# Second attention layer of a decoder: value products gathered at the end of a group, three dense PSUM banks in turn

## The chip, the cores and the metric

The kernel runs as one launch on one core of a Trainium2 chip. The core has a matrix engine (TensorE; PE for its matmuls, PEld for its weight loads), VectorE (DVE), ScalarE (ACT), GpSimd (POOL), SyncE (SP, which here starts DMAs), an on-chip memory of 128 partitions, and an accumulator memory, PSUM, with eight banks. The metric is device time in microseconds; lower is better.

## The reference, cut to what matters

A batch is 16 sequences of 224 rows of 512 numbers. Layer 1 is a quantised self-attention and layer 3 an attention with a mixture of experts; neither is touched. The change is all in layer 2, a cross attention of 16 heads of 32 over a context of 750 rows:

```python
q = (Q @ Wq + bq).reshape(B, L, H, E)      # B=16, L=224, H=16, E=32
k = (K @ Wk + bk).reshape(B, S, H, E)      # S=750, K = V = ctx_1024
v = (V @ Wv + bv).reshape(B, S, H, E)
scores = jnp.einsum('blhe,bshe->bhls', q, k)
A = jax.nn.softmax(scale * scores, axis=-1)
out = jnp.einsum('bhls,bshd->blhd', A, v).reshape(B, L, H * E)
return out @ We + be                        # then x = layernorm(x + that)
```

## The kernel before, in words

Layer 2 runs over the 16 batches in an unrolled loop. Each batch has four **groups** of four heads, since a head's 32 channels take a quarter of the 128 partitions. A group needs, on TensorE:

- four **row-max** products (`row_max`, L1439), each 112 queries by 376 keys for four heads into PSUM banks 0 to 3; VectorE reduces each to maxima (`reduce_max`, L1618). They are made one group ahead.
- the maxima transposed (unit M, L1370), copied by ScalarE (L1553).
- three **score** products (`scores`, L1449 and L1453), each 250 keys by 224 queries for four heads, into the same banks 0 to 3; ScalarE takes the exponential (L1583).
- three **value** products (`values`, L1461), which sum exponentials times value rows over the keys, and two **ones** products (`sums`, L1468), which sum the exponentials themselves after GpSimd has added them pairwise (L1347, L1352). Both go to bank 6 or 7, as the group is even or odd. VectorE then takes the reciprocal and multiplies (`attend`, L1630 and L1631) into `out_T`.

Row-max and score products share banks 0 to 3, so they alternate: row-max, VectorE reduces, scores, ScalarE exponentiates, row-max. While VectorE or ScalarE has those banks, TensorE does **dense** work of a neighbouring batch, set by hand in the table `WINDOWS`: C (transposes of 125 context rows, or of 112 rows of x for C6 and C7; eight a batch), Q (four), K (eight), VV (value rows, twelve), O (the output projection of the batch before; two of 112 rows by 512 columns). Dense units and M take banks 4 and 5 in turn by their place in `ORDER`. ScalarE copies a dense result (the high part for C, Q, K; all of it for VV), and VectorE then writes the low-order rest (`unit` in the vector block: C L1600, Q L1604, K L1608; O L1614). A unit waits until its bank's earlier unit has been emptied (`emptied`, `earlier_in_bank`).

One group on TensorE is: row-max 0, M, slot 0, the last ones product of the group before, then for t = 0, 1, 2: scores t, slot 2t+1, row-max t+1, slot 2t+2, values t; the first ones product follows values 2. A group so has seven slots of dense work.

`first()` makes everything of batch 0 ahead of the loop; `final()` makes the last output. In batch 0 there is no O, in batch 15 no work for a next batch. SyncE stores a finished batch, then loads the rows of the context and of x of a later batch, then the rows `y2` to which an output is added; all these go out in that order. GpSimd adds the bias row to `y2` at a batch's start (L1341).

## Time and profile before

| what | value |
|---|---|
| median of three timed runs | 4292.89 us (4291.1 to 4294.06) |
| the profiled execution | 4295.02 us, its span 4293.1 us |
| PE, PEld, DVE, ACT, POOL busy over the span | 81%, 58%, 59%, 38%, 20% |
| mean granted TensorE clock | 0.876 of full speed |
| batches of layer 2 | from some 1366 us to 2879 us of the span |

A PE row's duration runs from a matmul's start to its modelled end and overlaps the next row, so the cost of a stretch is read from start to start of neighbouring rows. "x16" means sixteen instructions merged in one row; a float32 product appears as two instructions. The names say what is written and read; Wv, Wk, Wq tell the units VV, K and Q apart.

### The profile page before, as it was taken

Reading aid. Unit: us, or ns where it says so; the run is one execution under the profiler, and the core shown is the slowest. Engines: PE = TensorE matmul, PEld = TensorE weight load, DVE = VectorE, ACT = ScalarE, POOL = GpSimd, SP = SyncE. Lnnn points to the kernel's source line nnn. Section 1 sums busy time; section 2 is a strip of 40 time slices with the busy share of each in tenths; the row PEclk is TensorE's granted clock in tenths of the full one; section 3 lists DMA queues with packets and bytes.
Section 4 is the critical chain, followed back from the end, with each engine's and each line's share of the span. In section 5 each row is a group of like instructions: output and inputs, shape, how many; then the busy total and the mean of one; then the engine's idle time right before and its main releaser. Section 6 shows DMA issues by size and latency. Waiting matters only on the chain. (4 is left out here: it accounts for less than half of the span.)

```text
span 4293.1 us, 76365 instructions
## 1 busy us (share of the span) xinstructions
PE 3463.3 (81%) x30658; PEld 2482.2 (58%) x30658; DVE 2514.2 (59%) x3799; ACT 1626.5 (38%) x3064; POOL 873.9 (20%) x710
## 2 busy tenths in 40 slices
PE   0787753279647999999999999959994299999994
PEld 0343321146226777777777777735552298999993
DVE  8679889989863555555555555527764133333333
ACT  2222279968023333333333333313221133333332
POOL 0000012200001333343333334320001411111110
PEclk9998875555778999999999999969996599999997
DMA  3500033333051110000111000012100533433325
GB/s 152 182 1 1 15 112 105 95 94 95 0 181 45 40 36 29 29 29 29 33 37 43 29 29 29 10 39 64 40 21 36 190 83 84 93 86 84 83 44 151
DMA packets 140172, 276.51 MB, mean 64 GB/s; under 512 B 43464, under 2 KB 43464, under 8 KB 135776
## 3 DMA queue, kind: packets, MB, share of 16 engines
q1 hardware_dynamic: 124208, 239.60, 17.7%
q0 software_dynamic: 14592, 30.44, 4.1%
q8 instruction: 234, 3.83, 0.4%
q10 hardware_dynamic: 1072, 2.10, 0.2%
q14 instruction: 66, 0.54, 0.0%
HBM read 158.02 MB, written 102.23 MB: 61 GB/s over the span
## 5 line engine op out<-in xcount | busy, mean ns | idle before, releaser
L1618 DVE TENSOR_REDUCE arena<-psum 112x4 f32<-112x1504 f32 x256 | 440.3, 1720 | 303.2 <-PE psum L1439 302.7
L1583 ACT ACTIVATE arena<-psum 125x1792 f32<-125x1792 f32 x192 | 320.3, 1668 | 289.3 <-PE psum L1453 289.3
L1347 POOL TENSOR_TENSOR arena<-arena 125x896 f32<-125x896 f32 x128 | 270.1, 2110 | 680.9 <-ACT arena L1583 680.9
L1352 POOL TENSOR_TENSOR arena<-arena 125x896 f32<-125x896 f32 x128 | 269.3, 2104 | 292.4 <-ACT arena L1583 287.4
L2367 POOL DMA_INDIRECT x_plus_h_rows<-arena x72 | 114.6, 1592 | 731.7 <-DVE arena L2538 727.4
L2528 DVE TENSOR_TENSOR gelu_T_rest<-arena,gelu_T_high 128x384 fp32r<-128x384 f32 (+1 forms) x192 | 104.6, 547 | 269.5 <-ACT gelu_T_high L2474 269.5
L2389 PE MATMUL psum<-tokens_T_high,w_high 128*128 128x384 f32 (+1 forms) x768 | 255.6, 333 | 1.6 <-DVE tokens_T_rest L2503 1.6
L2391 PE MATMUL psum<-tokens_T_high,w_rest 128*128 128x384 f32 (+1 forms) x768 | 254.9, 332 | 0.0
L2390 PE MATMUL psum<-tokens_T_rest,w_high 128*128 128x384 f32 (+1 forms) x768 | 254.7, 332 | 0.0
L1608 DVE SCALAR_TENSOR_TENSOR k_T_rest<-psum,arena,k_T_high 128x376 fp32r<-128x376 f32 x128 | 77.9, 609 | 287.1 <-ACT k_T_high L1564 287.1
L821 ACT ACTIVATE arena<-arena,scales 112x224 bf16<-112x224 uint8 x512 | 238.5, 467 | 2.5
L760 PE MATMUL psum<-arena 64*112 64x224 bf16 x512 | 79.2, 410 | 191.2 <-DVE arena L780 178.5
L1360 PE MATMUL psum<-Wv_high,ctx_T_high 128*125 128x256 f32 x768 | 231.3, 301 | 0.0
L2389 PE MATMUL psum<-w_high,gelu_T_high 128*128 128x512 f32 (+1 forms) x576 | 228.7, 397 | 0.0
L2469 ACT ACTIVATE arena<-psum 128x384 f32<-128x384 f32 (+1 forms) x192 | 92.6, 482 | 354.3 <-PE psum L2391 352.7
L2391 PE MATMUL psum<-w_high,gelu_T_rest 128*128 128x512 f32 (+1 forms) x576 | 224.9, 390 | 0.0
L2390 PE MATMUL psum<-w_rest,gelu_T_high 128*128 128x512 f32 (+1 forms) x576 | 224.3, 389 | 0.0
L1361 PE MATMUL psum<-Wv_rest,ctx_T_high 128*125 128x256 f32 x768 | 215.5, 281 | 0.0
L1362 PE MATMUL psum<-Wv_high,ctx_T_rest 128*125 128x256 f32 x768 | 215.5, 281 | 0.0
L1461 PE MATMUL psum<-arena 125*32 125x224 f32 x3072 | 190.9, 367 | 5.4 <-ACT arena L1583 5.4
L1360 PE MATMUL psum<-ctx_T_high,Wk_high 128*128 128x376 f32 x512 | 184.1, 360 | 0.0
L1361 PE MATMUL psum<-ctx_T_rest,Wk_high 128*128 128x376 f32 x512 | 171.2, 334 | 0.0
(361 smaller groups left out, 8680.8 us busy)
## 6 DMA issues: line engine op xcount, KB each, us to landing
arena<-L_ffn_moe_w SPq DMA_DIRECT2D x16, 2048.0 KB, 10.9
arena<-ctx SPq DMA_DIRECT2D x16, 1500.0 KB
rows_by_slot<-arena SPq DMA_DIRECT2D x1, 18200.0 KB, 52.1
arena<-x SPq DMA_DIRECT2D x14, 1024.0 KB, 13.1
arena<-arena SPq DMA_DIRECT2D x16, 896.0 KB, 7.0
arena<-x_after_attn SPq DMA_DIRECT2D x32, 448.0 KB, 16.2
dots_ints<-arena SPq DMA_DIRECT2D x16, 784.0 KB, 4.8
arena<-dots_ints SPq DMA_DIRECT2D x16, 784.0 KB, 5.7
```

The source lines that it names most:

```text
L821: last = S.activation(junk[:, pr % 2, j, :], d8[:, u, h, (j % 2) * NS:(j % 2 + 1) * NS], ACT.Exp, scale=col("minus_s_d")[0:HALF], accum_ou ...
L1347: G.tensor_tensor(some_exps[:, r, :, :], prob[:, t, :, 0:NS], prob[:, t, :, NS:2 * NS], ALU.add).then_inc(paired, 1)
L1352: G.tensor_tensor(some_exps[:, 0, :, :], some_exps[:, 0, :, :], prob[:, 1, :, s * NS:(s + 1) * NS], ALU.add).then_inc(paired, 1)
L1360: PE.matmul(to, wh(k), xh(k), start=(k == 0), stop=False)
L1361: PE.matmul(to, wh(k), xl(k), start=False, stop=False)
L1362: last = PE.matmul(to, wl(k), xh(k), start=False, stop=(k == KC - 1))
L1461: last = PE.matmul(psum[DH2 * j:DH2 * (j + 1), 6 + g % 2, 0:NS], vR[:, u, mt, h * DH2:(h + 1) * DH2], prob[:, t, j, s * NS:(s + 1) * NS], ...
L1583: S.activation(prob[:, t, :, :], score_psum(MC, 2 * NS), ACT.Exp, scale=SCALE2).then_inc(exp_done, 1)
L1618: return V.tensor_reduce(rmx[:, i // 2, i % 2, :], score_psum(HALF, HC), axis=AX.X, op=ALU.max).then_inc(r_free, 1)
L2389: PE.matmul(to, wh(k), xh(k), start=(k == 0), stop=False)
L2390: PE.matmul(to, wh(k), xl(k), start=False, stop=False)
L2391: last = PE.matmul(to, wl(k), xh(k), start=False, stop=(k == n - 1))
```

## The change

Value and ones products of a group all come after its last row-max product, in one run, into bank 6 for every group. Bank 7 joins 4 and 5 as a dense bank; a unit's bank is its place in `ORDER` modulo three, and a unit waits for the one three places earlier. `None` entries pad `ORDER` so that banks fit. A group has six slots; `WINDOWS` is rewritten so that each batch's same C, Q, K and VV units stand in them, and O is cut into four units of 112 rows by 256 columns, spread over groups 0 to 2. `out_T` is doubled, so that the next batch's groups don't overwrite what O still reads. On VectorE, `attend` comes ahead of slot 0's units, and a row maximum comes ahead of the rests of the slot before it (but behind an O); the three small operations of `combine` follow the last row maximum directly. GpSimd adds the bias row after its first addition of a batch. SyncE stores a batch when four O units are read, so after the last slot of group 2 of the next batch (before: slot 5 of group 0).

```diff
-        o2T = sb("out_T", [P, NG2, NS], F32, L2)
+        o2T = sb("out_T", [P, 2, NG2, NS], F32, L2)
...
+        NO2 = 4
         WINDOWS = (
-            (((Q, 3),), ((K, 6),), ((K, 7),), ((O, 0),), ((C, 0), (C, 1)), ((O, 1),), ((C, 2), (C, 3))),
-            (((C, 4), (C, 5)), ((K, 0),), ((C, 6), (C, 7)), ((K, 1),), ((VV, 0),), ((VV, 1), (VV, 2)), ((Q, 0),)),
-            (((Q, 1),), ((K, 2),), ((VV, 3),), ((K, 3),), ((VV, 4),), ((VV, 5),), ((VV, 6),)),
-            (((Q, 2),), ((K, 4),), ((VV, 7),), ((K, 5),), ((VV, 8),), ((VV, 9), (VV, 10)), ((VV, 11),)),
+            (((K, 6),), ((K, 7),), ((Q, 3), (C, 0)), ((O, 0),), ((VV, 0), (C, 1)), ((VV, 1), (C, 2))),
+            (((VV, 2), (C, 3)), ((O, 1),), ((VV, 3), (C, 4)), ((K, 0),), ((VV, 4), (C, 5)), ((VV, 5), (C, 6))),
+            (((VV, 6), (C, 7)), ((K, 1),), ((O, 2),), ((VV, 7), (Q, 0)), ((K, 2),), ((O, 3),)),
+            (((K, 3),), ((VV, 8), (Q, 1)), ((K, 4),), ((VV, 9), (Q, 2)), ((K, 5),), ((VV, 10), (VV, 11))),
         )
+        DENSE_BANKS = (4, 5, 7)
+        NDB = len(DENSE_BANKS)
+        VALUE_BANK = 6
...
         def bank(unit):
-            return 4 + ORDER.index(unit) % 2
+            return DENSE_BANKS[ORDER.index(unit) % NDB]
...
                         for g in range(NG2):
-                            last = PE.matmul(psum[0:HALF, at, :], o2T[:, g, i * HALF:(i + 1) * HALF], We[:, g, :], start=(g == 0), stop=(g == NG2 - 1))
+                            last = PE.matmul(psum[0:HALF, at, 0:DV2], o2T[:, u, g, rows], We[:, g, cols], start=(g == 0), stop=(g == NG2 - 1))
...
+                        def values_and_sums():
+                            pe.wait_ge(attended, n + 2)
+                            if g == 0:
+                                pe.wait_ge(v_moved, b * NV2 + NV2)
+                            for t in range(TP):
+                                pe.wait_ge(exp_done, n * TP + (t + 1))
+                                values(u, g, t)
+                            for r in range(ROUNDS):
+                                sums(n, g, r)
                         next_max(0)
                         dense((M, g), b, b_next, b_before, u, first, last)
                         slot(0)
-                        if not (first and g == 0):
-                            sums(n - 1, (g - 1) % NG2, 1)
                         for t in range(TP):
                             next_scores(t)
                             slot(2 * t + 1)
                             next_max(t + 1)
-                            slot(2 * t + 2)
-                            next_values(t)
+                            if t < TP - 1:
+                                slot(2 * t + 2)
+                        values_and_sums()
...
                         for t in range(TP):
-                            slot(2 * t + 1)
+                            of_output = [what for what in WINDOWS[g][2 * t + 1] if what[0] == O]
+                            others = [what for what in WINDOWS[g][2 * t + 1] if what[0] != O]
+                            empty(of_output)
                             if more:
                                 reduce_max(n + 1, t + 1)
-                            slot(2 * t + 2)
-                        if more:
-                            combine(n + 1, ch)
+                                if t == TP - 1:
+                                    combine(n + 1, ch)
+                            empty(others)
+                            if t < TP - 1:
+                                empty(WINDOWS[g][2 * t + 2])
```

TensorE at the end of a group, before: the last value product (L1461; waits for the exponential, x2_exp), the first ones product (L1468), row-max 0 (L1439), M (L1370).

```order
L1461 MATMUL psum<-arena 32x224 [waits x2_exp]
L1461 MATMUL psum<-arena 32x224 x7
L1468 MATMUL psum<-arena,ones 32x224 [waits x2_ps]
L1468 MATMUL psum<-arena,ones 32x224 x3
L1439 MATMUL psum<-k_T_high,q_T_high 112x376 [waits x2_rfr,x2_kmv,x2_qmv]
L1439 MATMUL psum<-k_T_high,q_T_high 112x376 x3
L1439 MATMUL psum<-k_T_rest,q_T_high 112x376 x4
L1439 MATMUL psum<-k_T_high,q_T_rest 112x376 x4
L1370 MATMUL psum<-identb,arena 128x112 [waits x2_nmx,x2_vmv]
L1370 MATMUL psum<-identb,arena 128x112
```

The same place in the change, from the first value product (L1477) on; L1484 is the ones product, L1455 the row-max.

```order
L1477 MATMUL psum<-arena 32x224 [waits x2_exp,x2_att]
L1477 MATMUL psum<-arena 32x224 x7
L1477 MATMUL psum<-arena 32x224 [waits x2_exp]
L1477 MATMUL psum<-arena 32x224 x7
L1477 MATMUL psum<-arena 32x224 [waits x2_exp]
L1477 MATMUL psum<-arena 32x224 x7
L1484 MATMUL psum<-arena,ones 32x224 [waits x2_ps]
L1484 MATMUL psum<-arena,ones 32x224 x3
L1484 MATMUL psum<-arena,ones 32x224 [waits x2_ps]
L1484 MATMUL psum<-arena,ones 32x224 x3
L1455 MATMUL psum<-k_T_high,q_T_high 112x376 [waits x2_rfr,x2_kmv,x2_qmv]
L1455 MATMUL psum<-k_T_high,q_T_high 112x376 x3
```

Value products 0 and 1 and the second ones product have moved here; they stand in one unbroken run.

TensorE ahead of scores 0, before: the last matmul of a Q unit (L1362), the second ones product (L1468), the scores (L1449).

```order
L1362 MATMUL psum<-x_T_high,Wq_rest 128x224
L1468 MATMUL psum<-arena,ones 32x224 [waits x2_ps]
L1468 MATMUL psum<-arena,ones 32x224 x3
L1449 MATMUL psum<-q_T_high,k_T_high 125x224 [waits x2_tmv,x2_rfr]
L1449 MATMUL psum<-q_T_high,k_T_high 125x224 x3
L1449 MATMUL psum<-q_T_rest,k_T_high 125x224 x4
```

The same place in the change: the last matmul of a K unit (L1377), the scores (L1465).

```order
L1377 MATMUL psum<-ctx_T_high,Wk_rest 128x376
L1465 MATMUL psum<-q_T_high,k_T_high 125x224 [waits x2_tmv,x2_rfr]
L1465 MATMUL psum<-q_T_high,k_T_high 125x224 x3
L1465 MATMUL psum<-q_T_rest,k_T_high 125x224 x4
L1465 MATMUL psum<-q_T_high,k_T_rest 125x224 x4
```

Scores now follow dense work directly, with no product in tiles of 32 columns between.

VectorE in group 3, before: row maximum L1618, rests of Q L1604 and K L1608, `attend` L1630 and L1631, `combine` L1623 to L1625.

```order
L1618 TENSOR_REDUCE arena<-psum 112x4 [waits x2_rmm]
L1604 SCALAR_TENSOR_TENSOR q_T_rest<-psum,arena,q_T_high 128x224 [waits x2_qhi]
L1630 RECIPROCAL arena<-psum 128x224 [waits x2_sum]
L1631 TENSOR_TENSOR arena<-psum,arena 128x224 [waits x2_dch]
L1608 SCALAR_TENSOR_TENSOR k_T_rest<-psum,arena,k_T_high 128x376 [waits x2_khi]
L1618 TENSOR_REDUCE arena<-psum 112x4 [waits x2_rmm]
L1608 SCALAR_TENSOR_TENSOR k_T_rest<-psum,arena,k_T_high 128x376 [waits x2_khi]
L1618 TENSOR_REDUCE arena<-psum 112x4 [waits x2_rmm] x2
L1623 TENSOR_TENSOR arena<-arena 112x8 [waits x2_rfr]
L1624 TENSOR_SCALAR arena<-arena 112x8 [waits x2_dch]
L1625 SCALAR_TENSOR_TENSOR arena<-arena 112x8 [waits x2_dch]
```

The same group in the change: row maximum L1636, `attend` L1648 and L1649, rests of K L1625 and Q L1621, `combine` from L1641.

```order
L1636 TENSOR_REDUCE arena<-psum 112x4 [waits x2_rmm]
L1648 RECIPROCAL arena<-psum 128x224 [waits x2_sum]
L1649 TENSOR_TENSOR arena<-psum,arena 128x224 [waits x2_dch]
L1625 SCALAR_TENSOR_TENSOR k_T_rest<-psum,arena,k_T_high 128x376 [waits x2_khi]
L1636 TENSOR_REDUCE arena<-psum 112x4 [waits x2_rmm]
L1621 SCALAR_TENSOR_TENSOR q_T_rest<-psum,arena,q_T_high 128x224 [waits x2_qhi]
L1625 SCALAR_TENSOR_TENSOR k_T_rest<-psum,arena,k_T_high 128x376 [waits x2_khi]
L1636 TENSOR_REDUCE arena<-psum 112x4 [waits x2_rmm]
L1621 SCALAR_TENSOR_TENSOR q_T_rest<-psum,arena,q_T_high 128x224 [waits x2_qhi]
L1625 SCALAR_TENSOR_TENSOR k_T_rest<-psum,arena,k_T_high 128x376 [waits x2_khi]
L1636 TENSOR_REDUCE arena<-psum 112x4 [waits x2_rmm]
L1641 TENSOR_TENSOR arena<-arena 112x8 [waits x2_rfr]
```

The row maximum has moved ahead of the rests that wait for ScalarE, `attend` ahead of the first rest.

## Rows read from the trace of the kernel before

**Rows 1.** windows view (us; busy PE, PEld, DVE, ACT, POOL; clock, DMA share, GB/s), second layer

```profile
2039.00:2146.00 107.00, 105.35 (x1320) 77.18 (x1316) 58.69 (x72) 41.57 (x57) 40.06 (x19) 1.00 0.11 33
```

**Rows 2.** timeline of ACT (start us, us, engine line op): two copies of group 0's maxima

```profile
1458.86 0.35 ACT L1553 COPY arena<-psum 128x224 bf16<-128x224 bf16 x1 [1.81 <-PE psum L1370]
...
2778.98 0.35 ACT L1553 COPY arena<-psum 128x224 bf16<-128x224 bf16 x1 [1.81 <-PE psum L1370]
```

**Rows 3.** timeline of PE from 2017 us: first instruction of each stretch

```profile
2017.02 0.38 PE L1360 MATMUL psum<-Wv_high,ctx_T_high 128*125 128x256 f32 x1
...
2020.06 0.43 PE L1439 MATMUL psum<-k_T_high,q_T_high 32*112 32x376 f32 x4
...
2020.77 0.38 PE L1360 MATMUL psum<-Wv_high,ctx_T_high 128*125 128x256 f32 x1
...
2022.37 0.96 PE L1461 MATMUL psum<-arena 125*32 125x224 f32 x16
2023.15 0.56 PE L1468 MATMUL psum<-arena,ones 125*32 125x224 f32 x8
2023.64 0.43 PE L1439 MATMUL psum<-k_T_high,q_T_high 32*112 32x376 f32 x4
...
2024.36 0.27 PE L1370 MATMUL psum<-identb,arena 112*128 112x112 bf16 x2
2024.44 0.35 PE L1360 MATMUL psum<-x_T_high,Wq_high 128*128 128x224 f32 x1
...
2025.95 0.58 PE L1468 MATMUL psum<-arena,ones 125*32 125x224 f32 x8
2026.47 0.37 PE L1449 MATMUL psum<-q_T_high,k_T_high 32*125 32x224 f32 x4
...
2027.51 0.44 PE L1360 MATMUL psum<-ctx_T_high,Wk_high 128*128 128x376 f32 x1
...
2029.76 0.43 PE L1439 MATMUL psum<-k_T_high,q_T_high 32*112 32x376 f32 x4
...
2034.65 3.69 PE L1403 MATMUL psum<-arena 128*112 128x512 f32 x8
2038.27 0.43 PE L1439 MATMUL psum<-k_T_high,q_T_high 32*112 32x376 f32 x4
...
2038.98 1.07 PE L1382 MATMUL psum<-ident,arena 125*128 125x125 f32 x8
2039.98 0.96 PE L1461 MATMUL psum<-arena 125*32 125x224 f32 x16
2040.87 0.38 PE L1449 MATMUL psum<-q_T_high,k_T_high 32*125 32x224 f32 x4
```

**Rows 4.** waits view, 1950 to 2136 us (us in total, times, longest)

```profile
PEld psum L1370 <- DVE ctx_T_rest L1600: 1.9, 2, 0.9
```

**Rows 5.** timeline of all engines, batch 0, a stretch after scores without dense work

```profile
1376.04 0.37 PE L1449 MATMUL psum<-q_T_high,k_T_high 32*125 32x224 f32 x4
...
1378.92 0.43 PE L1439 MATMUL psum<-k_T_high,q_T_high 32*112 32x376 f32 x4 [1.76 <-ACT arena L1583]
```

**Rows 6.** timeline of DVE, 2020 to 2031 us: a row maximum and a rest of K

```profile
2020.88 1.72 DVE L1618 TENSOR_REDUCE arena<-psum 112x4 f32<-112x1504 f32 x1 [5.17 <-PE psum L1439]
...
2030.48 0.61 DVE L1608 SCALAR_TENSOR_TENSOR k_T_rest<-psum,arena,k_T_high 128x376 fp32r<-128x376 f32 x1 [1.60 <-ACT k_T_high L1564]
```

**Rows 7.** page, part 5: the additions on POOL (xcount, busy, mean ns)

```profile
L1347 POOL TENSOR_TENSOR arena<-arena 125x896 f32<-125x896 f32 x128 | 270.1, 2110 | 680.9 <-ACT arena L1583 680.9
```

**Rows 8.** DMA view, 1948 to 2000 us (KB each, median us to landing)

```profile
arena<-x_after_attn SPq DMA_DIRECT2D x2, 448.0 KB, 15.8
xattn_rows<-arena SPq DMA_DIRECT2D x1, 448.0 KB, 3.1
```

**Rows 9.** timeline of PE, the second pair of transposes before batch 0

```profile
1308.20 1.93 PE L1382 MATMUL psum<-ident,arena 125*128 125x125 f32 x8 [0.55 <-DVE ctx_T_rest L1600]
```

**Rows 10.** windows view, the last batch, columns as in Rows 1

```profile
2804.00:2827.00 23.00, 16.24 (x210) 9.96 (x210) 8.86 (x10) 5.00 (x4) 8.37 (x4) 0.55 0.01 1
```

More of the change, by code:

```diff
@@ L1244, in bank @@
         def bank(unit):
-            return 4 + ORDER.index(unit) % 2
+            return DENSE_BANKS[ORDER.index(unit) % NDB]
         def earlier_in_bank(unit, first, last):
-            at = ORDER.index(unit) - 2
-            while at >= 0 and not present(ORDER[at], first, last):
-                at -= 2
+            at = ORDER.index(unit) - NDB
+            while at >= 0 and (ORDER[at] is None or not present(ORDER[at], first, last)):
+                at -= NDB
             if at >= 0:
@@ L1255, in earlier_in_bank, with last_in_bank @@
                 return None, 0
-            at = len(ORDER) + ORDER.index(unit) - 2 - 2 * (ORDER.index(unit) // 2)
+            at += len(ORDER)
+            assert ORDER[at] is not None and ORDER[at][0] != O
             return ORDER[at], 1
+        def last_in_bank(i):
+            at = len(ORDER) - NDB + i
+            while ORDER[at] is None or not present(ORDER[at], False, True):
+                at -= NDB
+            return ORDER[at]
         with phase("x2", "c", "x", "y0", "y1", "yb", "cmm", "chi", "clo", "qmm", "qhi", "qmv", "kmm", "khi", "kmv", "vmm", "vmv", "rmm", "rfr", "nmx", "tmm", "tmv",
@@ L1430, in dense @@
                         emptied(*earlier, batch_of(earlier, b_before, b, b_next))
-                    unit(kind, i, bank(what), batch_of(what, b_before, b, b_next), u)
+                    unit(kind, i, bank(what), batch_of(what, b_before, b, b_next), 1 - u)
                 def row_max(g, i):
@@ L1467, in sums @@
                     for j in range(GH):
-                        last = PE.matmul(psum[DH2 * j:DH2 * (j + 1), 6 + g % 2, NS:2 * NS], ones[0:MC, 0:DH2], some_exps[:, r, j, :],
+                        last = PE.matmul(psum[DH2 * j:DH2 * (j + 1), VALUE_BANK, NS:2 * NS], ones[0:MC, 0:DH2], some_exps[:, r, j, :],
                                          start=False, stop=(r == ROUNDS - 1))
@@ L1539, in final @@
                 def final():
-                    sums(NB * NG2 - 1, NG2 - 1, 1)
-                    for i in range(2):
-                        if i == 0:
-                            pe.wait_ge(o_read, 2 * NB - 2)
-                            pe.wait_ge(t_moved, NB * NG2)
-                        unit(O, i, 4 + i, NB - 1, 1)
+                    for i in range(NO2):
+                        if i < NDB:
+                            earlier = last_in_bank(i)
+                            emptied(*earlier, batch_of(earlier, NB - 2, NB - 1, None))
+                        else:
+                            emptied(O, i - NDB, NB - 1)
+                        unit(O, i, DENSE_BANKS[i % NDB], NB - 1, 1)
                 loop(pe, first, body, final)
@@ L1584, in body @@
                             slot(2 * t + 1)
-                            slot(2 * t + 2)
+                            if t < TP - 1:
+                                slot(2 * t + 2)
                 def first():
                     for i, (kind, j) in enumerate(FIRST):
-                        unit(kind, j, 4 + i % 2, 0, 0)
+                        unit(kind, j, DENSE_BANKS[i % NDB], 0, 0)
                 loop(act, first, body, lambda: None)
@@ L1637, in body, with empty @@
                         ch = Chain(dve, dch, n * 3 + 2) if not first or g else Chain(dve, dch, 2)
-                        def slot(i):
-                            for what in WINDOWS[g][i]:
+                        def empty(some):
+                            for what in some:
                                 if present(what, first, last):
@@ L1664, in first @@
                     for i, (kind, j) in enumerate(FIRST):
-                        unit(kind, j, 4 + i % 2, 0, 0)
+                        unit(kind, j, DENSE_BANKS[i % NDB], 0, 0)
                     for i in range(4):
@@ L1671, in final @@
                     dve.wait_ge(attended, NB * NG2 + 1)
-                    attend(NB * NG2 - 1, NG2 - 1, Chain(dve, dch, (NB * NG2 - 1) * 3 + 3))
-                    for i in range(2):
-                        unit(O, i, 4 + i, NB - 1, 1)
+                    attend(NB * NG2 - 1, NG2 - 1, 1, Chain(dve, dch, (NB * NG2 - 1) * 3 + 3))
+                    for i in range(NO2):
+                        unit(O, i, DENSE_BANKS[i % NDB], NB - 1, 1)
                 loop(dve, first, body, final)
```

48 lines of the change are left out of this document (22 added, 26 removed).

## The prediction

> **What bounds the kernel now.** I read the windows first. Inside layer 2 TensorE is busy 105.35 of 107 us at granted clock 1.00, while VectorE has 58.69, ScalarE 41.57 and GpSimd 40.06 [rows 1]. So a middle batch lasts as long as TensorE's own work, its changes from one kind of product to another, and what it waits for. Next the timeline of ScalarE gives the length of a batch: its copies of the maxima of group 0 lie at 1458.86 (batch 1) and 2778.98 (batch 15), so the 14 batches between take 94.29 us each [rows 2]. Then TensorE's timeline, from start to start [rows 3]: a stretch of two VV 3.04, of one 1.60; K 2.25; Q 1.51; two C 1.00; O 3.62; row-max 0.71; M 0.08; scores 1.04; values 0.89 when scores follow and 0.78 when ones follow; ones 0.49 behind values and 0.52 alone.
>
> The second VV costs 1.44, so opening and closing a dense stretch costs 3.04 - 2 x 1.44 = 0.16. Without it a unit costs K 2.09, Q 1.35, C 0.42, O 3.46. A batch of before is then: 8 K 16.72, 12 VV 17.28, 4 Q 5.40, 8 C 3.36, 2 O 6.92, 4 M 0.32, 16 row-max 11.36, 12 scores 12.48, the values and ones of four groups 4 x (0.89 + 0.89 + 0.78 + 0.49 + 0.52) = 14.28, and 28 dense stretches x 0.16 = 4.48; together 92.60. The measured 94.29 leaves 1.69 us of waits. The waits view shows the largest: twice in two batches the M of group 1 stands 0.95 us behind VectorE's rest of a C unit, its bank's earlier user [rows 4].
>
> **The change part by part, in a middle batch.**
>
> Dense stretches. They go from 28 to 24: 4 x 0.16 = -0.64. The number of K, VV, Q and C units is the same. A stretch that now touches scores directly (12 a batch) has no example in a steady batch; dense next to values and dense next to row-max cost alike, so I take the same 0.16. Its bounds are 0.08 (half a change) and 0.24, thus 1.0 us a batch either way.
>
> Values and ones. In one run they pay for one opening and one closing. Closing towards scores is 0.89 - 0.78 = 0.11, so eight ones instructions without it are 0.49 - 0.11 = 0.38 and sixteen values instructions in the middle of a run 0.76. The run is 0.78 + 0.76 + 0.76 + 0.38 + 0.49 = 3.17 against 3.57: four groups -1.60. Bounds are 3.0 (ones as short as the rows' overlap would let them be) and 3.57 (nothing saved).
>
> O. Its columns stay the same, its instructions go from 16 to 32. A VV instruction of 256 columns takes 1.44 / 12 = 0.12, of which 0.107 are its columns at 2.4 GHz; 16 more at 0.013 are +0.2. The page "TensorEngine Tiling (Array Packing)" of the Trainium skill, section "Instruction Overhead", has about 60 cycles on each matmul; as an estimate by that rule the sixteen would add 0.4 us, and the end would be 3 us later than mine. VV's step contradicts 60 cycles on top of the columns, so I don't use it.
>
> The old waits. 1.69 goes, if three banks remove it. With two banks a unit waits for the one two before; M of group 1 stood directly behind a pair of C. With three, and with C never next to C, each unit's predecessor has at least one whole stretch of banks 0 to 3 between. So -1.69, with bounds 0 and -1.69.
>
> New waits. Two floors must be covered by every dense stretch. After scores: with no dense work scores to row-max takes 2.88 [rows 5], less 1.04 leaves 1.84. After row-max: the reduction starts 0.82 after the products and lasts 1.72 [rows 3, 6], so scores can follow 2.54 after row-max began, less 0.71 leaves 1.83. The thinnest stretches now are an O quarter, 3.46 / 2 + 0.2 / 4 + 0.16 = 1.94, Q3 with C0, 1.93, and VV with C, 2.02: all above both floors, but by 0.1. This holds only if the reduction starts at once. Before, it could stand behind a rest that waits for ScalarE (0.61 for K [rows 6]); it now comes ahead of these. That delays the emptying: the rest of K7 ends 2.54 + 0.61 = 3.15 after row-max 1 began and O0, which takes its bank, starts at 0.71 + 1.93 + 1.04 = 3.68. V5 behind the rest of K0 is the same case. I allow +0.1 for all of it.
>
> The run of values waits for nothing new: the third exponential ends before row-max 3. Its second ones product needs an addition on GpSimd (2.11 [rows 7]) which starts when that exponential ends; TensorE comes to it 0.71 + 0.78 + 1.52 + 0.38 = 3.4 later, so 1.2 us are spare. The reduction of row-max 3 (2.54) hides beneath the run, and so do the three small operations ahead of M. `attend` (reciprocal and product, unchanged) comes earlier by one rest, and delays only that rest, whose bank is asked for three units later.
>
> The queues. O3 is read about 62 us into a batch (by the prices above, groups 0 and 1 take 43 and group 2 up to its last slot 19); only then SyncE stores, issues the context and x loads that stand behind, and last y. The store lands in 3.1 and the loads of x and y in 15.8 [rows 8], so y is there some 20 us later. GpSimd asks for it about 36 us after O3: 28 to the end of the batch, then row-max, M, K6, scores, the exponential and one addition of 2.11. The next C needs its rows at about the same time. Cost 0, with 16 us to spare.
>
> Sum of a middle batch: -0.64 - 1.60 + 0.2 - 1.69 + 0.1 = -3.63; 14 of them -50.8.
>
> The ends. Before batch 0, transposes in pairs wait 0.55 for a bank three times [rows 9]; with three banks that goes: -1.7. Batch 0 has no O. Before, its two empty O stretches shrank from 3.62 to the floor, 3.5 us; now four stretches of 1.94 shrink by 0.1 each. So it gains almost nothing more than 3.63 - 3.5 and I take -0.5. Batch 15 has hardly any dense work, and TensorE's granted clock there is 0.55 [rows 10], near its lower level of 1.2 GHz. At the full clock: O leaves two waits of group 0 that it overfilled, -3.5; the values of three groups, which lay in time that was empty anyway, are now 3.17 in a lump instead of 1.27, +5.7; in group 3 two value products (0.89) leave the chain between exponentials, -1.8; sum +0.4. At the half clock the four O quarters overfill their waits by 1.8 each and the lumps double: up to +12. I take +2.
>
> Total: -50.8 - 0.5 - 1.7 + 2 = -51. From the profiled execution's own 4295.02 that is 4244.0. That execution stands 2.1 above the median of the timed runs (4292.89), so I say **4242 us**.
>
> **The rivals.**
>
> A, *the banks come back too late*. For it: row maxima now go first on VectorE, the stretches stand 0.1 above the floors, O0 and V5 have 0.5 to spare. Against it: ScalarE and VectorE are idle more than half of the time. If three places a batch wait 0.5 each, that is 1.5 x 14 = 21: 4263.
>
> B, *the run saves nothing*: the change from one kind of product to another is inside a value product anyway, and the ends of dense stretches toward scores cost more. Then only the waits go: 1.69 x 14 + 2 = 26, 4268. Against it: 0.78 against 0.89 is there in every group.
>
> C, *the second ones product stands on GpSimd*. Place: the end of each group. Before, a whole dense stretch lay between its addition and its product; now 1.2 us do. For it: in group 0 GpSimd has the bias row to add too. Against it: about 6.5 us lie between two exponentials, GpSimd has at most 4.3 of additions in that time. It turns the sum when GpSimd is late by more than 1.2 + 3.6 / 4 = 2.1 in each group; at 3 late the batch loses 7.2, less 3.6 is +3.6 x 14 = 50 above the median of before: 4343, slower.
>
> D, *y comes too late* for GpSimd, which holds all additions behind it. It costs nothing below 36 us from O3 to landing, turns the sum at 40; at 45 a batch loses 9 - 3.6, so +75 on the median of before: 4368. Against it are the 20 us above.
>
> **How the numbers follow.** Forecast 0.66; A 0.17; B 0.08; C 0.05; D 0.02; all rest 0.02. The boundary of dense and scores (1.0 a batch, 14 us), the ends (-3 to +12) and A's sum make the range: low 4225 (all boundaries cheap), high 4266. A measurement of this kernel can tell 0.2% from no change, 8.6 us. Forecast, A and B are all faster by more; a mixture of B with a slow batch 15 comes near zero. Faster 0.88, same 0.05, slower 0.07.
>
> **What would show it.** Right: batches of about 90.7 us between the copies of group 0's maxima; a run of values and ones of some 3.2 from its first start to row-max 0; M directly behind row-max in each group; no wait of L1385 on a rest; dense stretches with K 2.25 as before, beside scores too. A is right if TensorE's weight loads of O, VV or scores wait on VectorE's rests or reductions; B if the run takes 3.5 or K before scores 2.4; C if ones (L1484) wait for GpSimd; D if GpSimd's first long idle of a batch ends at a DMA. I am wrong in the main if batches stay above 92.5.

## The result, and the profile after

| kernel | median, us | lowest to highest | against before |
|---|---|---|---|
| before | 4293.48 (4 runs) | 4291.1 to 4295.32 | |
| changed | 4236.80 (4 runs) | 4233.41 to 4245.45 | ratio 0.9874, 95% interval 0.9861 to 0.9886 |

The change saves 56.7 us, 1.3%. The prediction said 4242, with a range of 4225 to 4266. The spans of the profiled executions are 4293.1 and 4236.8, apart by 56.3.

The windows view of the changed kernel, the stretch that answers to [rows 1]:

```profile
2039.00:2146.00 107.00, 107.00 (x1421) 87.09 (x1420) 59.10 (x73) 43.14 (x59) 40.80 (x20) 1.00 0.10 29
```

TensorE has no idle time left there: 107.00 of 107 us busy at clock 1.00, against 105.35. The timeline of ScalarE, copies of group 0's maxima (L1569 now), answers to [rows 2]; the first is batch 0's:

```profile
1360.57 0.35 ACT L1569 COPY arena<-psum 128x224 bf16<-128x224 bf16 x1 [13.22 <-PE psum L1385]
...
1458.66 0.35 ACT L1569 COPY arena<-psum 128x224 bf16<-128x224 bf16 x1 [4.41 <-PE psum L1385]
...
2724.73 0.35 ACT L1569 COPY arena<-psum 128x224 bf16<-128x224 bf16 x1 [4.41 <-PE psum L1385]
```

Batches 1 to 14 take (2724.73 - 1458.66) / 14 = 90.43 us each; before 94.29, foretold 90.66. TensorE's timeline, the end of group 0 and the start of group 1 of such a batch, answers to [rows 3] (L1375 dense, L1397 transposes C, L1465 scores, L1455 row-max, L1477 values, L1484 ones, L1385 M, L1419 O):

```profile
1922.45 0.39 PE L1375 MATMUL psum<-Wv_high,ctx_T_high 128*125 128x256 f32 x1
...
1923.98 0.59 PE L1397 MATMUL psum<-ident,arena 125*128 125x125 f32 x4
1924.50 0.38 PE L1465 MATMUL psum<-q_T_high,k_T_high 32*125 32x224 f32 x4
...
1925.54 0.39 PE L1375 MATMUL psum<-Wv_high,ctx_T_high 128*125 128x256 f32 x1
...
1927.08 0.59 PE L1397 MATMUL psum<-ident,arena 125*128 125x125 f32 x4
1927.60 0.43 PE L1455 MATMUL psum<-k_T_high,q_T_high 32*112 32x376 f32 x4
...
1928.30 2.48 PE L1477 MATMUL psum<-arena 125*32 125x224 f32 x48
1930.60 0.94 PE L1484 MATMUL psum<-arena,ones 125*32 125x224 f32 x16
1931.47 0.43 PE L1455 MATMUL psum<-k_T_high,q_T_high 32*112 32x376 f32 x4
...
1932.17 0.27 PE L1385 MATMUL psum<-identb,arena 112*128 112x112 bf16 x2
1932.26 0.36 PE L1375 MATMUL psum<-Wv_high,ctx_T_high 128*125 128x256 f32 x1
...
1933.76 0.59 PE L1397 MATMUL psum<-ident,arena 125*128 125x125 f32 x4
1934.28 0.37 PE L1465 MATMUL psum<-q_T_high,k_T_high 32*125 32x224 f32 x4
...
1935.32 1.98 PE L1419 MATMUL psum<-arena 128*112 128x256 f32 x8
1937.23 0.43 PE L1455 MATMUL psum<-k_T_high,q_T_high 32*112 32x376 f32 x4
```

VV with C takes 2.05 (1922.45 to 1924.50), dense next to scores costs no more than next to row-max (2.06 from 1925.54 to 1927.60), an O quarter 1.91, the run of values and ones 3.17 (1928.30 to 1931.47). M follows row-max after 0.70. No start stands behind a wait. In the waits view of two batches what is left of VectorE's reductions is

```profile
PEld psum L1465 <- DVE arena L1636: 2.0, 10, 0.3
```

Before, the same view (1950 to 2136 us) had 22 such entries:

```profile
PEld psum L1449 <- DVE arena L1618: 8.3, 22, 0.6
```

These are waits of weight loads, and most of them cost nothing: the pieces' sum left only 1.69 us a batch for all waits.

Where the 56.3 us of span went, from the rows that mark the ends (TensorE's first transposes at 1305.71 and 1303.87, the last store's issue at 2878.72 and 2822.66):

| stretch | before | changed | difference | foretold |
|---|---|---|---|---|
| up to layer 2's first transpose | 1305.71 | 1303.87 | -1.8 | 0 |
| to batch 0's copy of maxima | 60.59 | 56.70 | -3.9 | -1.7 |
| batch 0 | 92.56 | 98.09 | +5.5 | -0.5 |
| batches 1 to 14 | 1320.12 | 1266.07 | -54.1 | -50.8 |
| batch 15 to the last store | 99.74 | 97.93 | -1.8 | +2 |

The 0.2 us that are missing to 56.3 lie behind layer 2. The first line is code that the change doesn't touch; in the eleven experiments below it lies between 1.2 us above before and 6.2 us below, so it is noise. So runs are compared below by the length of their own stretches.

### The profile page after: what moved, and what is told of

Its sections match the earlier page's. It is cut to its first block and busy times, and to the rows that moved or that the text cites. A ratio compares the mean times of both kernels' runs of the same rounds, so it can differ in the third digit from the quotient of the medians.

```text
span 4236.8 us, 76941 instructions
## 1 busy us (share of the span) xinstructions
PE 3414.0 (81%) x30914; PEld 2544.5 (60%) x30914; DVE 2515.7 (59%) x3831; ACT 1629.3 (38%) x3064; POOL 873.8 (21%) x710
## 5 line engine op out<-in xcount | busy, mean ns | idle before, releaser
L1636 DVE TENSOR_REDUCE arena<-psum 112x4 f32<-112x1504 f32 x256 | 441.6, 1725 | 531.0 <-PE psum L1455 531.0
L1359 POOL TENSOR_TENSOR arena<-arena 125x896 f32<-125x896 f32 x128 | 269.8, 2108 | 830.6 <-ACT arena L1599 637.5
L1599 ACT ACTIVATE arena<-psum 125x1792 f32<-125x1792 f32 x192 | 320.3, 1668 | 160.7 <-PE psum L1469 160.7
L1375 PE MATMUL psum<-Wv_high,ctx_T_high 128*125 128x256 f32 x768 | 233.0, 303 | 0.0
L1377 PE MATMUL psum<-Wv_high,ctx_T_rest 128*125 128x256 f32 x768 | 217.0, 283 | 0.0
L1375 PE MATMUL psum<-ctx_T_high,Wk_high 128*128 128x376 f32 x512 | 183.4, 358 | 0.0
L760 PEld LDWEIGHTS psum<-arena 64*112 64x112 bf16 x512 | 34.2, 187 | 236.4 <-DVE arena L780 223.2
L1377 PE MATMUL psum<-ctx_T_high,Wk_rest 128*128 128x376 f32 x512 | 171.2, 334 | 0.0
```

Source lines behind the costliest of these rows:

```text
L1359: G.tensor_tensor(some_exps[:, r, :, :], prob[:, t, :, 0:NS], prob[:, t, :, NS:2 * NS], ALU.add).then_inc(paired, 1)
L1375: PE.matmul(to, wh(k), xh(k), start=(k == 0), stop=False)
L1377: last = PE.matmul(to, wl(k), xh(k), start=False, stop=(k == KC - 1))
L1599: S.activation(prob[:, t, :, :], score_psum(MC, 2 * NS), ACT.Exp, scale=SCALE2).then_inc(exp_done, 1)
L1636: return V.tensor_reduce(rmx[:, i // 2, i % 2, :], score_psum(HALF, HC), axis=AX.X, op=ALU.max).then_inc(r_free, 1)
```

## The experiments

All times "batch" are the mean of batches 1 to 14 by the same two copies of maxima. Before is 94.29, the changed kernel 90.43.

**e1, two dense banks.**

```diff
-        DENSE_BANKS = (4, 5, 7)
+        DENSE_BANKS = (4, 5)
```

> The changed kernel with two dense banks (4 and 5) in turn instead of three; order, values in one run and O in quarters stay. Theory: three banks matter at two places of a middle batch, read from the changed kernel's trace: C0 would stand behind the rest of K7 (ends 1919.2, C0 starts 1918.28: about 1.0 us) and C5 behind the rest of K0 (ends 1946.3, C5 starts 1945.51: about 0.9). So a middle batch goes from 90.43 to 92.3 us, and the transposes before batch 0 from 7.8 to 10.8; 4236.8 + 14 x 1.9 + 3 = about 4267. Rival: the new order alone took the waits away, the third bank does nothing in the loop: batch 90.4, total about 4240. Second rival: every unit meets a wait somewhere, batch 94 or more, total above 4285.

Measured: 4268.93 us (ratio to before 0.994, 0.9924 to 0.9957), batch 92.42, +1.99. The waits view of two batches, weight loads of the transposes:

```profile
PEld psum L1397 <- DVE k_T_rest L1625: 3.8, 4, 1.0
```

Four waits of 0.95 in two batches, all of C units behind rests of K, as the theory named them (C0 behind K7, C5 behind K0).

**e2, value products apart.** `next_values(t)` makes value product t, and behind the third both ones products (before, the second of them stood behind slot 0 of the next group).

```diff
                             next_max(t + 1)
                             if t < TP - 1:
                                 slot(2 * t + 2)
-                        values_and_sums()
+                            next_values(t)
```

> The changed kernel with value products 0 and 1 put back behind slots 2 and 4, value product 2 and both ones products at the end; three banks and six slots stay. Theory (a change between kinds of product costs what the rows say): each of the two costs 0.89 instead of 0.76, so +0.13 x 8 = +1.0 a middle batch, 91.5 us; the last batch gains some 5 since two of its value products again lie in empty time; about 4236.8 + 15 - 5 = 4247. Rival B of the prediction (a run saves nothing): batch 90.4, about 4232. Rival: the run's place, not its length, matters (a reduction or exponential was hidden less well before), batch above 92.5.

Measured: 4278.35 us (ratio 0.9958, 0.9944 to 0.9972), batch 93.24, +2.81 and not +1.0. TensorE's timeline at the end of group 1 of a middle batch (L1455 row-max, L1477 values, L1484 ones), and VectorE's beneath it (L1637 row maximum):

```profile
1970.57 0.43 PE L1455 MATMUL psum<-k_T_high,q_T_high 32*112 32x376 f32 x4
...
1971.28 0.96 PE L1477 MATMUL psum<-arena 125*32 125x224 f32 x16
1972.06 1.19 PE L1484 MATMUL psum<-arena,ones 125*32 125x224 f32 x16
1973.27 0.43 PE L1455 MATMUL psum<-k_T_high,q_T_high 32*112 32x376 f32 x4
```

```profile
1971.40 1.72 DVE L1637 TENSOR_REDUCE arena<-psum 112x4 f32<-112x1504 f32 x1 [3.25 <-PE psum L1455]
```

Three value products cost 0.89 + 0.89 + 0.78 = 2.56 in place of 2.30, the +1.04 a batch that the theory had. But ones now take 1.21 (1972.06 to 1973.27) in place of 0.87: row-max 0 may start only when the reduction of row-max 3 has ended, at 1971.40 + 1.72 = 1973.12, and 0.78 + 0.87 don't cover it. That is 0.34 to 0.36 in each group, 1.4 a batch. Another 0.3 stands behind M of group 2. The new table has no slot behind row-max 3, so the run at the end is what hides that reduction; its place weighs as much as its being one piece. So the theory and its last rival both hold a part.

**e3, the kernel before with three dense banks.**

```diff
-            return 4 + ORDER.index(unit) % 2
+            return DENSE_BANKS[ORDER.index(unit) % NDB]
...
-                                pe.wait_ge(attended, n + 1)
+                                pe.wait_ge(attended, n + 2)
```

`DENSE_BANKS` is (4, 5, 7), and values and ones of every group go to bank 6, so value product 0 now waits for the `attend` of the group before (second edit).

> The kernel before with dense banks 4, 5 and 7 in turn and bank 6 for all values; its order, seven slots and VectorE order stay. Theory: of the 1.69 us of waits a batch only those on a bank go: M of group 1 (0.7 more than usual) and the transposes behind it (0.2 to 0.4), so a batch of 93.2 us; what stays is 0.24 at a lone VV after scores (the exponential's floor) and 0.21 where a reduction stands behind rests. Prologue 3 shorter. 4293.5 - 14 x 1.1 - 3 = about 4275. Rival: all waits were bank waits, batch 92.6, about 4267. Second rival: single value bank makes value product 0 wait for attend: batch above 94.3.

Measured: 4285.65 us (ratio 0.9975, 0.9965 to 0.9985), batch 94.07, only -0.22. TensorE's timeline, row-max 0 and M (L1383) of group 1:

```profile
1951.04 0.43 PE L1452 MATMUL psum<-k_T_high,q_T_high 32*112 32x376 f32 x4
...
1952.46 0.26 PE L1383 MATMUL psum<-identb,arena 112*128 112x112 bf16 x2 [0.65 <-DVE arena L1637]
```

M starts 1.42 after row-max 0, where 0.71 is normal, as before, and what it waits for is L1637, the last operation of `combine`, not a bank. The theory is refuted: the largest old wait was VectorE's order. The third bank does take away the waits at the C units of group 1, but behind C6 and C7 the scores now wait for a row maximum (L1630), which stands behind other work of VectorE:

```profile
1960.33 0.37 PE L1462 MATMUL psum<-q_T_high,k_T_high 32*125 32x224 f32 x4 [0.42 <-DVE arena L1630]
```

**e4, the changed kernel with VectorE's order of before** (`combine` stays behind the last row maximum; the first line of the edit stands ahead of `attend`).

```diff
+                        empty(WINDOWS[g][0])
...
-                            empty(of_output)
+                            empty(WINDOWS[g][2 * t + 1])
                             if more:
                                 reduce_max(n + 1, t + 1)
...
-                            empty(others)
```

> The changed kernel with VectorE's order of before: a slot's rests ahead of the row maximum that follows it, attend behind the rests of slot 0. Theory: where K stands in the slot after scores its rest ends about 0.45 later than the reduction could start; that shows where the next stretch is thin: Q3 with C0, O2, VV4 with C5, 0.2 to 0.4 each, so about +0.9 a batch, 91.3, total about 4250. Rival: the stretches cover it, batch 90.4, total 4237. Second rival: attend's delay holds a bank and M or K wait, batch above 92.5.

Measured: 4253.43 us (ratio 0.9907, 0.9891 to 0.9924), batch 91.43, +1.00. Q3 with C0 takes 2.30 in place of 1.96. O2 takes 2.31 (from 1964.25) in place of 1.91, and the scores behind it wait for the row maximum:

```profile
1966.56 0.38 PE L1465 MATMUL psum<-q_T_high,k_T_high 32*125 32x224 f32 x4 [0.33 <-DVE arena L1636]
```

VV4 with C5 takes 2.31 in place of 2.06. All three places and sizes are those expected.

**e5, all three undone: the table of six slots is left** (edits of e1, e2 and e4 together, and `combine` last; O stays in quarters, and both ones products stay behind value product 2).

> The changed kernel with only its new table of six slots (and O in quarters, out_T doubled, GpSimd's order) left: two dense banks, value products 0 and 1 apart, VectorE's order of before, combine last. Theory (the three aids each carry weight only because the stretches are thinner): undone one by one they cost 1.99, 2.81 and 1.00 us a middle batch; together 90.43 + 5.8 = about 96.2, slower than the 94.29 of before, total about 4325. Rival (each aid saves by itself, six slots save their 0.64 in any case): batch 93 to 94, total 4275 to 4290.

Measured: 4286.94 us (ratio 0.9987, 0.9978 to 0.9997), batch 93.80. The theory is refuted, the costs don't add: undone alone they are 1.99, 2.81 and 1.00, together 3.37. Next to e2 the banks and VectorE's order are worth only 93.80 - 93.24 = 0.56. TensorE's rows show why. VectorE's old order writes the rest of K ahead of the row maximum, so C0 behind K7 and C5 behind K0 start at once with two banks too: Q3 ahead of C0 takes 1.44, where in e1 it took 2.42 with the wait. The row maxima that this delays lie ahead of scores 1 and 2, beneath a value product of 0.89. What is left stands at the end of groups 0 and 1, where a rest of C goes ahead of the reduction of row-max 3. Timeline of TensorE and of VectorE at the end of group 0:

```profile
1948.67 1.18 PE L1484 MATMUL psum<-arena,ones 125*32 125x224 f32 x16
1950.36 0.43 PE L1455 MATMUL psum<-k_T_high,q_T_high 32*112 32x376 f32 x4 [0.52 <-DVE arena L1637]
```

```profile
1947.91 0.68 DVE L1618 TENSOR_TENSOR ctx_T_rest<-psum,ctx_T_high 128x500 fp32r<-128x500 f32 x1 [3.29 <-ACT ctx_T_high L1574]
1948.50 1.71 DVE L1637 TENSOR_REDUCE arena<-psum 112x4 f32<-112x1504 f32 x1
```

The ones take 1.69 here and 1.60 in group 1, against 1.21 to 1.23 in e2 and 0.87 in the changed kernel. The 94.29 - 93.80 = 0.49 that e5 saves against before is a balance: four stretches fewer -0.64, ones in one piece -0.56 (4 x (1.01 - 0.87)), the old waits -1.69, O in quarters +0.08, the ones' new waits +2.25; together -0.56.

**e6, the kernel before with `combine` directly behind the last row maximum.**

```diff
                                 reduce_max(n + 1, t + 1)
+                                if t == TP - 1:
+                                    combine(n + 1, ch)
                             slot(2 * t + 2)
-                        if more:
-                            combine(n + 1, ch)
```

> The kernel before with one edit: the three small operations of combine stand directly behind the last row maximum, ahead of the rests of slot 6. Theory: the 0.7 us that M of group 1 waited was for these, behind the rests of C2 and C3, not for a bank; group 0 to 1 goes from 25.55 to about 25.0 with two banks (M then waits for its bank's rest of C2, some 0.15), a batch 93.8, total about 4287. Rival (the prediction's reading, a bank wait): no change, 94.3.

Measured: 4291.42 us (ratio 0.9993, 0.9984 to 1.0003, which is no difference that the times can show); batch 94.16. TensorE's timeline at the same place:

```profile
1952.81 0.43 PE L1439 MATMUL psum<-k_T_high,q_T_high 32*112 32x376 f32 x4
...
1953.66 0.27 PE L1370 MATMUL psum<-identb,arena 112*128 112x112 bf16 x2
1954.24 1.07 PE L1382 MATMUL psum<-ident,arena 125*128 125x125 f32 x8 [0.31 <-DVE ctx_T_rest L1600]
```

M starts 0.85 after row-max 0 and not 1.41, and from group 0's M to group 1's it is 25.00 in place of 25.55, as the theory said. But C4 behind it waits 0.31 for the rest of its bank's C unit, and the next group is 0.43 longer (23.29 against 22.86). Here two waits lay over one another: the order of VectorE and the bank. Removing the first shows the second.

**e7, the first row-max products between the value rows.** Before batch 0 each of group 0's four row-max products stands ahead of three VV.

```diff
                     for i, (kind, j) in enumerate(FIRST):
+                        if kind == VV and j % (NV2 // 4) == 0:
+                            m = j // (NV2 // 4)
...
+                            row_max(0, m)
```

> The changed kernel with another order before batch 0: the four row-max products of group 0 stand each ahead of three VV units instead of behind all twelve. Theory: three reductions of 2.54 us, which left TensorE idle, go beneath the VV units: -9.5; and TensorE's clock, which fell in that idle time (K6 of batch 0 took 3.41 instead of 2.24), stays up: -1.5 more. Total 4236.8 - 11 = about 4226, middle batches 90.43. Rival: batch 0 waits for something else anyway (table load of the exponential, ScalarE's copies), total about 4232.

Measured: 4228.28 us (ratio 0.9849, 0.9833 to 0.9866), 8.5 below the changed kernel's median. From the first transpose to the copy of maxima 49.6 in place of 56.7: -7.1, less than the 9.5. (The intervals of the two ratios touch; it is this stretch that tells the kernels apart.) Batch 0 didn't gain, 98.45: K6 took 2.24, but group 0's ones products now waited for GpSimd twice, 1.65 and 1.45, where the changed kernel waits 1.44 once, and the clock fell behind that.

**e8, the bias row back at the head of a batch** (GpSimd's order of before).

> The changed kernel with GpSimd's addition of the bias row back at the head of a batch. Theory: GpSimd's first tensor operation of the layer starts some 7 us after it could (in batch 0 the first addition of exponentials began at 1374.5, its exponential ended at 1367.4); at the head of batch 0 this is hidden as before, so ones 2 of group 0 doesn't wait 1.4 and VectorE's small operation of 2.02 takes 0.2: batch 0 shorter by 1.5 to 2, middle batches 90.43, total 4235. Rival: y now is asked for before it has landed in every batch, batches above 91.

Measured: 4235.42 us (ratio 0.9869, 0.9852 to 0.9885), batch 0 97.92, middle batches 90.43. Ones 2 of group 0 no longer waits, yet batch 0 loses 0.2 us and not 1.5 to 2. In this profiled run the clock fell once more, right behind the empty O place of group 1 (VV took 2.72 in place of 1.54; the granted clock from 1390 to 1394 us is 0.57, where the changed kernel has 1.00). y is never late.

**e9, the value products of the last batch alone apart.**

> The changed kernel with value products 0 and 1 of the last batch alone back behind slots 2 and 4 (the other batches keep their run). Theory: in batch 15 the slots are nearly empty, so the two products lie in time in which TensorE waits, and the run that three groups put on the chain (3.3 us at half clock) shrinks; -5, total about 4232. Rival: the short run leaves the last reduction bare and the clock falls further, 4236 to 4240.

Measured: 4240.65 us (ratio 0.9876, 0.9861 to 0.9892), not told apart from the changed kernel. Batch 15 to the last store is 94.90 in place of 97.93, -3.0 and not -5; batch 0, untouched, was 101.3 in this profiled run in place of 98.1. So in total it is inconclusive, and the mechanism shows in its own stretch. The 101.3 also says how far a length of batch 0 can be trusted: the same code took 98.1 in one profiled execution and 101.3 in another, so the 0.2 of e8 and the 1.0 of e10 below are no differences by themselves.

**e10, batch 0's empty O places filled** with products of We that nobody reads.

```diff
                         def slot(i):
+                            if first and not any(present(w, first, last) for w in WINDOWS[g][i]):
+                                what = WINDOWS[g][i][0]
...
+                                count = 1 if last and i % 2 == 0 else 3
+                                for k in range(count):
+                                    PE.matmul(psum[0:HALF, bank(what), 0:DV2], We[:, k, 0:HALF], We[:, k, 0:DV2], start=(k == 0), stop=(k == count - 1))
```

> The changed kernel with each of batch 0's four empty O places filled by three float32 products of We with itself (256 columns, about 1.4 us, read by nobody, overwritten by the bank's next unit). Theory: batch 0 takes 98.1 against 90.4 of a middle batch because TensorE's idle 1.8 us at these places lets the granted clock fall (VV 2.61 instead of 1.53, values 3.72 instead of 2.30); filled, batch 0 takes 93.5 to 94.5, total about 4233. Rival: the floors and GpSimd's late start make it, and filling changes nothing or adds: 4237 to 4239.

Measured: 4240.09 us (ratio 0.9884, 0.9868 to 0.9899), batch 0 97.06, -1.0. By itself it does nothing that the times show. But the filling does what it was meant to do, and GpSimd takes the gain away. Windows view of e10 behind the ones products of group 0 and at the O place of group 2 (1417 us), where the changed kernel's clock is 0.57:

```profile
1387.00:1390.00 3.00, 3.00 (x24) 2.55 (x19) 2.13 (x2) 0.34 (x1) 0.00 (x0) 0.50 0.03 5
1417.00:1421.00 4.00, 3.64 (x50) 3.00 (x49) 1.80 (x2) 1.50 (x1) 0.52 (x1) 1.00 0.58 183
```

The clock no longer falls at the O places, and the value products of group 2 take 2.29. It falls in group 0, where TensorE now waits for GpSimd twice (3.39 us in all, against 1.44 once):

```profile
1384.18 0.58 PE L1484 MATMUL psum<-arena,ones 125*32 125x224 f32 x8 [1.94 <-POOL arena L1367]
1386.22 0.59 PE L1484 MATMUL psum<-arena,ones 125*32 125x224 f32 x8 [1.45 <-POOL arena L1359]
```

So the rival's number came out, but not its reason.

**e11, all of e7 to e10, and batch 15's empty slots filled as well.**

> First maxima between the values, bias row first, values of the last batch apart, and empty slots filled with such products of We in batch 0 and batch 15 (three after scores, one after row-max). Theory: -8.5 (run e7) - 1.4 (e8) - 4 (batch 0 at full clock) - 5 (e9) and in batch 15 the half clock goes, 3.12 + 3.74 per pair of row-max and scores becomes 2.6 + 2.9, some 1.4 x 11 = -15: about 4203. Rival: the fillers stand in the chain and the clock does not rise: above 4222.

Measured: 4213.00 us (ratio 0.9816, 0.9803 to 0.9830), 23.8 below the changed kernel. Batch 0 takes 90.61, batch 15 to the last store 85.65, middle batches 90.43. The windows view (columns as in [rows 1]) of batch 0 and batch 15, of the changed kernel and then of e11:

```profile
1361.00:1459.00 98.00, 89.07 (x1162) 72.73 (x1162) 48.07 (x56) 37.72 (x50) 35.93 (x17) 0.94 0.07 22
2725.00:2823.00 98.00, 71.05 (x877) 49.45 (x875) 36.13 (x42) 22.70 (x19) 35.69 (x17) 0.77 0.02 6
```

```profile
1355.00:1445.00 90.00, 88.43 (x1180) 72.01 (x1172) 46.78 (x55) 37.61 (x50) 36.02 (x17) 1.00 0.07 24
2721.00:2807.00 86.00, 66.26 (x848) 42.81 (x840) 29.78 (x35) 20.61 (x15) 31.84 (x17) 0.95 0.09 23
```

The granted clock is 1.00 in place of 0.94 in batch 0 and 0.95 in place of 0.77 in batch 15. In batch 0 the parts need each other: e7, e8 and e10 alone each left a fall of the clock, in e7 and e10 behind the waits for GpSimd that e8's order removes, in e8 behind the empty O places that e10 fills. Which smaller set would be enough wasn't run.

## Why the prediction was right, point by point

- *Dense stretches*, -0.64. Dense next to scores costs what dense elsewhere does, 0.09 to 0.10 at each end; VV with C 2.05 against the 2.02 used. The term was not measured by itself; e5's balance fits with it to 0.07.
- *Values and ones*, -1.60. The run takes 3.17, to the hundredth the sum of its pieces. The prediction names that the reduction of row-max 3 hides beneath the run, but gives it no price: with the run in pieces it is bare, 1.4 us a batch (e2).
- *O*, +0.2. A quarter takes 1.91 against 1.94; four of them 7.64 against 7.24 for two halves, 0.32 of which are the two more stretches, so +0.08. An O instruction of 256 columns takes (1.91 - 0.16) / 8 = 0.219 us, half of the 0.43 of one of 512, so nearly all of it goes by columns. The rule of about 60 cycles on each matmul (the Trainium skill, "TensorEngine Tiling (Array Packing)", section "Instruction Overhead"), read as the prediction read it, on top of the columns, makes +0.4 as an estimate; the measured +0.08 decides against that reading.
- *The old waits*, -1.69: the size holds, since nothing is left of them, but the step's reason failed, and that the number fits all the same is luck. The prediction read [rows 4], a wait of M's weight load on its bank, and gave the whole credit to the third bank. The row of M's matmul in the same trace of before names another:

```profile
1955.63 0.26 PE L1370 MATMUL psum<-identb,arena 112*128 112x112 bf16 x2 [0.64 <-DVE arena L1625]
```

M waited for `combine`, which stood behind the rests of C2 and C3, with a bank wait hidden just beneath (e6); the third bank alone gives 0.22 (e3). By TensorE's rows in a batch of before, 1.56 of the 1.69 stood at four places: 0.71 at this M, 0.18 at the C units behind it, 0.42 at C6 and C7 and the value product behind them, and 0.25 at a lone VV behind scores, whose stretch of 1.60 is shorter than its floor. In e5, with two banks, VectorE's old order and `combine` last, the only starts that wait in the middle batch read (1922 to 2018 us) are those of row-max 0: it is the new table that takes the old waits away. The third bank is worth 1.99 for another reason: it removes waits that the new table makes under VectorE's new order (e1).
- *New waits*, +0.1: none. The floor after scores held (2.88 less 1.04 in batch 0). The one after row-max came out at 1.90 and not 1.83 (row-max at 1413.32 to scores at 1415.93 over the empty O2 place of batch 0, 2.61 less 0.71), so O2 with its 1.91 covers it by 0.01 and not by 0.1; that nothing waits there is close to luck. e4 shows that they bind as soon as a reduction starts 0.4 late. Rival A is thus right in its mechanism and wrong in this kernel, because VectorE's new order prevents it.
- *Queues*. y and the context rows were in time in all batches; rival D is out. Rival C happened once, in batch 0: timeline of ScalarE, of GpSimd and of TensorE (L1599 exponential, L1359 addition, L1484 ones).

```profile
1365.70 1.67 ACT L1599 ACTIVATE arena<-psum 125x1792 f32<-125x1792 f32 x1
```

```profile
1374.53 2.10 POOL L1359 TENSOR_TENSOR arena<-arena 125x896 f32<-125x896 f32 x1 [193.16 <-issue]
...
1383.16 2.08 POOL L1359 TENSOR_TENSOR arena<-arena 125x896 f32<-125x896 f32 x1
```

```profile
1385.29 0.58 PE L1484 MATMUL psum<-arena,ones 125*32 125x224 f32 x8 [1.44 <-POOL arena L1359]
```

GpSimd's first addition starts 7.2 us after the exponential ended at 1367.37, and its last one so late that the second ones product waits 1.44.

- *The ends* are where the numbers were wrong. The way to batch 0 gained 3.9 and not 1.7: from the first transpose to Q0 went from 10.80 to 7.79. The prediction added up three idle entries of 0.55 [rows 9], but such an entry starts at the modelled end of a matmul, which overlaps the next; from start to start a pair had taken 2.49 (1308.20 less 1305.71), and from the first start to the modelled end of the last all eight units took 9.4 before and take 6.4 now. Batch 0 was forecast by its floors alone, at one clock; this is the step that was wrong in size and in kind. By its rows, against a middle batch of 90.43, it takes 1.6 more at K6 and K7 (3.41 and 2.67), whose clock fell while TensorE waited for the reductions ahead of batch 0, 1.6 at the ones product that waits for GpSimd, and 4.7 in the work right behind three of the four empty O places (before there were two places), where the clock is 0.57 to 0.59. e10 confirms the last term: with these places filled the clock stays at 1.00 there. TensorE's timeline, group 2 of batch 0:

```profile
1427.32 0.43 PE L1455 MATMUL psum<-k_T_high,q_T_high 32*112 32x376 f32 x4 [1.77 <-ACT arena L1599]
...
1428.21 3.90 PE L1477 MATMUL psum<-arena 125*32 125x224 f32 x48
1431.93 0.93 PE L1484 MATMUL psum<-arena,ones 125*32 125x224 f32 x16
```

The value products take 3.72 (1428.21 to 1431.93) where 2.30 is normal, directly after an idle 1.77. Batch 15 came out 1.8 better and not 2 worse. Its +2 was set between a sum at the full clock and one at the half clock, and the half clock was read from 23 us [rows 10]; over the whole batch the mean granted clock was 0.73 (2779 to 2879 us) and is now 0.77. How its terms came out one by one wasn't measured.

The total, -56 for -51, is right because the middle batch is (90.43 for 90.66), and this because its pieces were read from start to start and because the old waits did go, though by other parts of the change. The misses are -3.3 in the middle batches, -2.2 before batch 0, +6.0 in it, -3.8 in batch 15 and behind it, and -1.8 of noise ahead of the layer: 5 in sum, though one of them is 6: the ends cancel by luck.

## What to carry to other kernels

When an engine is full, price each change between kinds of work from start to start of neighbouring rows: a sum of such pieces foretold a batch to 0.3%. A weight load and its matmul wait separately, so read both rows before naming a wait's cause; even then a second wait can lie right under the first, and only changing one of them shows it. Aids against waits (a bank, an order, cover) aren't additive: what each is worth depends on which of the others are there. And a loop's first and last passes, emptied of their work, can lose to the clock what the steady passes gain.

## What the runs showed that was not expected

- GpSimd's first tensor operation of the layer starts late, and the trace shows behind what. Just ahead of it its sequencer has two MODIFY_POOL_CONFIG of the same line. View of L1359 of the changed kernel, 1360 to 1380 us, and of L1355, the bias row, in e8, 1300 to 1320 us:

```profile
L1359 POOLq MODIFY_POOL_CONFIG  x2: 11/11/11, 1367.6 to 1367.6; - x2
```

```profile
L1355 POOLq MODIFY_POOL_CONFIG  x2: 11/11/11, 1304.4 to 1304.4; - x2
```

The tensor operation starts 6.9 us later in both (1374.53 and 1311.27). In all thirteen kernels this first distance in the layer is 6.8 to 7.6 us; the same pair stands once in every two batches afterwards, with 0.1 us to the next operation. So whatever operation comes first pays. With the bias row ahead of batch 0, as in before and in e8, it is paid while GpSimd has nothing else to do, and the first addition of exponentials starts 0.2 us behind its exponential. What the chip does in the 7 us isn't in the rows.
- A VectorE operation on a 112 x 8 tile, 0.18 us elsewhere, took 2.02 in batch 0, while GpSimd's addition of 2.08 ran from 1383.16:

```profile
1383.26 2.02 DVE L1642 TENSOR_SCALAR arena<-arena 112x8 bf16<-112x8 f32 x1
```

It isn't the only one. In the kernel before, such an operation in 15 of the 16 batches began beneath the addition of the bias row and ended with it; VectorE's row and GpSimd's:

```profile
1551.13 1.15 DVE L1623 TENSOR_TENSOR arena<-arena 112x8 f32<-112x8 f32 x1
```

```profile
1549.87 2.40 POOL L1341 TENSOR_TENSOR arena<-arena 112x1024 f32<-112x1024 f32 x1 [0.30 <-issue]
```

The thirteen traces have 2496 of these three small operations in the layer. The 2406 with no addition of GpSimd beside them took at most 0.20 us. Of the 90 with one, 88 ended within 0.05 us of an addition's end, whatever was left of it, and the other two ran in the gap of 0.1 us between two additions. So the hold is shown; what the two engines share isn't.
- With its idle time filled TensorE's clock stayed at its upper level in batch 0 and until 2788 us in batch 15 (1.00 from 1355 to 1445 and from 2721 to 2788 us in e11), which was worth 7.5 and 12.3 us there together with the other edits. How much of the 12.3 is clock alone and how much the value products' place (3.0 in e9) wasn't separated further.
